# Moving the making of attention operand pieces from VectorE to GpSimd in a four-layer transformer kernel

## The reference

```
q, k, v = split of x @ w                        # per attention, heads of 8 features
s = q @ k^T (scaled)                            # attention 1 causal, 2 with distance slopes,
p = exp(s - max(s))                             # 3 with one more "void" key
y = (p @ v) / sum(p)
x = layernorm(x + y @ w_out)                    # float32 throughout
```

## Time and profile before

| | before |
|---|---|
| median of 3 runs | 1156.0 us |
| profiled execution | 1151.48 us, span 1149.7 us |
| PE busy | 981.2 us (85%) |
| DVE busy | 780.3 us (68%) |
| ACT busy | 660.3 us (57%) |
| POOL busy | 352.5 us (31%) |
| 12 first subtractions on DVE (L1557) | 14.9 us, 1240 ns each |
| 12 casts on DVE (L1559) | 9.3 us, 773 ns each |
| 12 second subtractions on DVE (L1561) | 14.7 us, 1226 ns each |

### The profile page before, as it was taken

One profiled execution on the slowest core, in us unless ns is written; L12 is line 12 of the kernel. 1 busy time (PEld: TensorE's weight loads), 2 busy tenths in 40 slices (PEclk: granted clock), 3 DMA queues, 4 the chain that ended last, 5 costly groups with the idle time before them and its releaser, 6 DMA issues.

```text
span 1149.7 us, 18859 instructions
## 1 busy us (share of the span) xinstructions
PE 981.2 (85%) x6456; PEld 500.3 (44%) x6517; DVE 780.3 (68%) x1663; ACT 660.3 (57%) x1282; POOL 352.5 (31%) x541
## 2 busy tenths in 40 slices
PE   5599779999887799446999999898899998888992
PEld 2266544445445588422333333476322222225661
DVE  5976596767752401389788887346988888855875
ACT  4755636665565254152677677584277766685451
POOL 7625510111342335520000001131021222645764
PEclk9799889999999899776999999989699999998996
DMA  5920224343631220233333210002334432411332
GB/s 141 175 68 1 69 84 162 122 134 111 152 88 47 59 60 25 62 102 130 98 121 129 77 63 31 2 1 82 106 105 147 133 103 78 112 29 47 97 102 84
DMA packets 98375, 101.70 MB, mean 88 GB/s; under 512 B 13354, under 2 KB 80571, under 8 KB 98199
## 3 DMA queue, kind: packets, MB, share of 16 engines
q1 hardware_dynamic: 86169, 89.28, 26.7%
q0 software_dynamic: 6432, 8.18, 2.5%
q10 hardware_dynamic: 5680, 3.04, 1.0%
HBM read 66.60 MB, written 38.09 MB: 91 GB/s over the span
## 4 chain that ended last, share of the span: by engine, by line
PE 66%; DVE 17%; ACT 6%; issue 5%; DMA 3%; POOL 2%; SPq 0%; another core or an unknown queue 0%; ACTq 0%; POOLq 0%; DVEq 0%
PE PS L894 13%; PE PS L878 12%; PE PS L851 8%; DVE negm L1696 6%; PE PS L705 5%; PE PS L700 5%; PE PS L1063 3%; PE PS L1073 3%; PE PS L881 3%; PE PS L1193 3%; PE PS L854 2%; PE PS L902 2%; ACT arena L1323 2%; PE PS L1208 2%; ACT arena L1250 2%
## 5 line engine op out<-in xcount | busy, mean ns | idle before, releaser
L1323 ACT ACTIVATE arena<-PS 128x512 f32<-128x512 f32 (+3 forms) x768 | 362.3, 549 | 185.5 <-PE PS L881 118.6
L1696 DVE TENSOR_REDUCE negm<-PS 128x2 f32<-128x1024 f32 (+3 forms) x384 | 404.5, 1087 | 88.1 <-PE PS L851 46.1
L878 PE MATMUL PS<-arena 128*128 128x512 bf16 (+3 forms) x707 | 218.7, 361 | 8.6 <-ACT arena L1323 5.4
L894 PE MATMUL PS<-arena,VPAD 128*32 128x512 f32 (+3 forms) x1536 | 186.3, 556 | 0.1
L851 PE MATMUL PS<-arena 32*128 32x512 bf16 (+3 forms) x768 | 143.9, 374 | 33.2 <-DVE negm L1696 28.1
L851 PEld LDWEIGHTS PS<-arena 32*128 32x128 bf16 x768 | 36.3, 91 | 215.0 <-DVE negm L1696 112.2
L878 PEld LDWEIGHTS PS<-arena 128*128 128x128 bf16 x768 | 69.7, 98 | 117.9 <-issue 54.2
L2533 POOL CAST nmp<-negm 128x16 bf16<-128x16 f32 x48 | 9.3, 195 | 360.1 <-DVE negm L1696 240.3
L700 PE MATMUL PS<-arena,W 128*128 128x512 f32 x144 | 81.4, 698 | 10.9 <-ACT arena L1241 8.5
L705 PEld LDWEIGHTS PS<-W,arena 128*128 128x128 f32 x640 | 79.6, 203 | 13.4 <-issue 6.7
L705 PE MATMUL PS<-W,arena 128*128 128x128 f32 x640 | 81.4, 288 | 3.3 <-DVE arena L1640 3.0
(11 more groups left out here) (335 smaller groups left out, 1538.8 us busy)
## 6 DMA issues: line engine op xcount, KB each, us to landing
arena<-score_q SPq DMA_DIRECT2D x48, 288.0 KB
arena<-score_k SPq DMA_DIRECT2D x48, 288.0 KB
arena<-max_parts SPq DMA_DIRECT2D x48, 256.0 KB
max_parts<-arena SPq DMA_DIRECT2D x36, 256.0 KB, 2.9
score_k<-arena SPq DMA_DIRECT2D x36, 128.0 KB
score_q<-arena SPq DMA_DIRECT2D x12, 384.0 KB
arena<-rows_y SPq DMA_DIRECT2D x16, 256.0 KB, 4.1
arena<-slots SPq DMA_DIRECT2D x46, 65.0 KB, 1.9
```

Source lines behind the costliest of these rows:

```text
L878: mm = pe.matmul(PS[:, b, q0:S], OK[s][:, r, kt * P:(kt + 1) * P], OQ[s][:, r, q0:S], start=True, stop=True)
L894: mm = pe.matmul(PS[32 * r:32 * r + 32, 7, q0:S], VP[:, u, kt, r, :], PB[:, kt % 2, r, q0:S], start=(kt == 0), stop=True, skip_group_check ...
L1323: act.activation(PB[:, kt % 2, r, q0:S], PS[:, 4 + use % 3, q0:S], ACT.Exp, scale=slope(u % G, r) if o["slope"] else 1.0).then_inc(exped, 1)
L1696: vec.tensor_reduce(negm[:, u % 2, 2 * rp:2 * rp + 2, qt], PS[:, 2 * (use % 2):2 * (use % 2) + 2, 0:nk], AX.X, ALU.max, negate=True).then_ ...
```

## The change

The three instructions of `splits` are made by GpSimd for chunks 1, 2 and 3 of every attention. Chunk 0's stay on VectorE. In GpSimd's stream chunk 1's three come in front of the first slots of lead, behind the last layer norm's roots. Those of chunks 2 and 3 come at slots 5, 7, 13 (chunk 2) and 15, 21, 23 (chunk 3). SP's spills and GpSimd's bias additions now wait on GpSimd for chunks 1 to 3.

```diff
+SPLIT_SLOTS = {5: (2, "lo"), 7: (2, "mid"), 13: (2, "low"), 15: (3, "lo"), 21: (3, "mid"), 23: (3, "low")}
...
-LAYER0_GPSIMD_TURNS = "01230130213020R011212323RR3RRRRRRR"
+LAYER0_GPSIMD_TURNS = "01230130213020R011212323RR31RRRRRRR023"
...
             def max_spills(c, tag, a):
-                sp.wait_ge(*V.at(c, tag + ".mid"))
+                sp.wait_ge(*(PO if c else V).at(c, tag + ".mid"))
...
             def score_spills(c, tag, a):
-                sp.wait_ge(*V.at(c, tag + ".low"))
+                sp.wait_ge(*(PO if c else V).at(c, tag + ".low"))
...
                     elif step == "split":
-                        splits(c, "p1")
+                        if c == 0:
+                            splits(c, "p1")
...
+            def split_low(c, tag):
+                L = lanes[c]
+                pool.wait_ge(*A.at(c, tag + ".k"))
+                pool.tensor_tensor(L.pair, L.pair, L.parts[:, :, 0, :], ALU.subtract).then_inc(*PO.did(c, tag + ".lo"))
+
+            def split_middle(c, tag):
+                L = lanes[c]
+                pool.wait_ge(*PO.at(c, tag + ".lo"))
+                pool.tensor_copy(L.parts[:, :, 1, :], L.pair).then_inc(*PO.did(c, tag + ".mid"))
+
+            def split_last(c, tag):
+                L = lanes[c]
+                pool.wait_ge(*PO.at(c, tag + ".mid"))
+                pool.tensor_tensor(L.parts[:, :, 2, :], L.pair, L.parts[:, :, 1, :], ALU.subtract).then_inc(*PO.did(c, tag + ".low"))
+
+            def first_splits(c, tag):
+                if c == 1:
+                    split_low(c, tag)
+                    split_middle(c, tag)
+                    split_last(c, tag)
...
+                    if t in SPLIT_SLOTS:
+                        c, piece = SPLIT_SLOTS[t]
+                        {"lo": split_low, "mid": split_middle, "low": split_last}[piece](c, f"p{a + 1}")
```

More of the change, by code:

```diff
@@ L92, in numbered @@
     return " ".join(f"{name}{i}" for i in range(n))
+SPLIT_STEPS = words(" ".join(f"p{a}.lo p{a}.mid p{a}.low" for a in (1, 2, 3)))
+SPLIT_SLOTS = {5: (2, "lo"), 7: (2, "mid"), 13: (2, "low"), 15: (3, "lo"), 21: (3, "mid"), 23: (3, "low")}
 NORM_V = "{0}.bn {0}.mv {0}.ln"
@@ L114 @@
 GPSIMD_STEPS = words(" ".join([
-    "m.va m.rs m.va2 m.rs2 m.lva m.lrs t.va t.rt t.rs t.s2 t.s1 t.va2 t.rt2 t.rs2 t.lva t.lrs o1.lva o1.lrs",
-    "x0.id x1.id cb.lva cb.lrs o2.xb o2.lva o2.lrs ch.xb ch.lva ch.lrs o3.xb r3.id r3.lva r3.lrs r3.nm r3.nb o3.lva o3.lrs r3.sh e.lva e.lrs"]))
+    "m.va m.rs m.va2 m.rs2 m.lva m.lrs t.va t.rt t.rs t.s2 t.s1 t.va2 t.rt2 t.rs2 t.lva t.lrs p1.lo p1.mid p1.low o1.lva o1.lrs",
+    "x0.id x1.id cb.lva cb.lrs p2.lo p2.mid p2.low o2.xb o2.lva o2.lrs ch.xb ch.lva ch.lrs p3.lo p3.mid p3.low o3.xb r3.id r3.lva r3.lrs r3.nm r3.nb o3.lva o3.lrs r3.sh e.lva e.lrs"]))
 TENSOR_STEPS = words(" ".join([
@@ L143 @@
 LAYER0_VECTOR = words("ss xn decay memory y x1 ss2 xn2 tot ln t.xn ssp t.tot t.ln split values")
-LAYER0_GPSIMD = words("rs rs2 lrs hh t.rs2 t.lrs")
+LAYER0_GPSIMD = words("rs rs2 lrs hh t.rs2 t.lrs split")
 LAYER0_TENSOR_TURNS = "0002300313202301332120112311001003201313131230102023220201310132121201202332011331RRR2RR2R2RR3R3RRRR3R"
@@ L153 @@
 COMBINE_VECTOR, COMBINE_VECTOR_TURNS = words("tot ln split values"), "010313021201RR3RRRRRRRR32RRR2R"
-COMBINE_GPSIMD, COMBINE_GPSIMD_TURNS = words("rs"), "R0RR132RRRRRRR"
+COMBINE_GPSIMD, COMBINE_GPSIMD_TURNS = words("rs split"), "R0RR1321RRRRRRR023"
 LAYER2_TENSOR, LAYER2_TENSOR_TURNS = words("o.tr o.out c.tr c.s c.out p.tr p.qk p.v p.vs"), "13103202110302312020101310021RR2R3RRRR2R3RRR3R32RR"
@@ L157 @@
 LAYER2_VECTOR, LAYER2_VECTOR_TURNS = words("o.tot o.ln c.tot c.ln split values scores"), "1310203211002021310103RRRRRR2R2RRR3R323RRR"
-LAYER2_GPSIMD, LAYER2_GPSIMD_TURNS = words("o.rs c.xb c.rs"), "103201120RRR233RRRRRRR"
+LAYER2_GPSIMD, LAYER2_GPSIMD_TURNS = words("o.rs c.xb c.rs split"), "103201120RRR2331RRRRRRR023"
 def rest(turns):
@@ L166, with __init__ @@
 class Steps:
-    def __init__(self, sem, engine, chunk_steps, whole_steps, last_only=()):
+    def __init__(self, sem, engine, chunk_steps, whole_steps, last_only=(), split=range(B)):
         self.sems = [sem(f"{engine}_chunk{c}") for c in range(B)] + [sem(f"{engine}_whole")]
-        self.order = [[name for name in chunk_steps if c == B - 1 or name not in last_only] for c in range(B)] + [whole_steps]
+        self.order = [[name for name in chunk_steps if (c == B - 1 or name not in last_only) and (c in split or name not in SPLIT_STEPS)]
+                      for c in range(B)] + [whole_steps]
         self.number = [{name: i + 1 for i, name in enumerate(steps)} for steps in self.order]
@@ L206, in sem @@
             return ctx.enter_context(nc.semaphore(name))
-        V = Steps(sem, "vector", VECTOR_STEPS, VECTOR_WHOLE, words("x1.y0 x1.y1 x1.y2"))
+        V = Steps(sem, "vector", VECTOR_STEPS, VECTOR_WHOLE, words("x1.y0 x1.y1 x1.y2"), range(1))
         A = Steps(sem, "scalar", SCALAR_STEPS, SCALAR_WHOLE)
-        PO = Steps(sem, "gpsimd", GPSIMD_STEPS, GPSIMD_WHOLE)
+        PO = Steps(sem, "gpsimd", GPSIMD_STEPS, GPSIMD_WHOLE, (), range(1, B))
         T = Steps(sem, "tensor", TENSOR_STEPS, TENSOR_WHOLE, words("o1.tr o1.out r1.tr r1.lg x1.o0 x1.o1 x1.o2 o3.tr o3.out r3.tr r3.lg"))
@@ L2009, in combine_and_prep @@
                     elif step == "split":
-                        splits(c, "p2")
+                        if c == 0:
+                            splits(c, "p2")
                     else:
@@ L2033, in layer2 @@
                     elif step == "split":
-                        splits(c, "p3")
+                        if c == 0:
+                            splits(c, "p3")
                     elif step == "values":
@@ L2370, in layer0 @@
                         root_of_sum(c)
+                    elif step == "split":
+                        first_splits(c, "p1")
                     else:
@@ L2439, in combine @@
                         continue
-                    norm(c, "cb")
+                    if step == "split":
+                        first_splits(c, "p2")
+                    else:
+                        norm(c, "cb")
             def layer2(slot):
                 for c in range(B):
-                    pool.wait_ge(*V.at(c, "p2.low"))
+                    pool.wait_ge(*(PO if c else V).at(c, "p2.low"))
                     biased(c, "o2", b2p)
@@ L2449, in layer2 @@
                         continue
-                    if step == "o.rs":
+                    if step == "split":
+                        first_splits(c, "p3")
+                    elif step == "o.rs":
                         norm(c, "o2")
@@ L2490, in inside3 @@
                 if t in BIAS_SLOTS:
-                    pool.wait_ge(*V.at(BIAS_SLOTS[t], "p3.low"))
+                    pool.wait_ge(*(PO if BIAS_SLOTS[t] else V).at(BIAS_SLOTS[t], "p3.low"))
                     biased(BIAS_SLOTS[t], "o3", b3o)
```

## The result

The changed kernel is not faster, it is a little slower. Its median was 1157.7 us (1154.49 to 1163.45, 11 runs) beside 1154.58 us for the kernel before (1147.19 to 1157.81, 11 runs): ratio 1.0047, 95% interval 1.0026 to 1.0067. Run again on another chip, it was 1180.11 against 1177.21 us, ratio 1.0025 (1.0002 to 1.0049). Later experiments ran on three chips, called by their numbers on record: 4, 9 and 5. On chips 9 and 5 the stretch behind attention 3 took 145 to 147 us in every profile; on chip 4 and in the first result it took 130 to 131 us. So times are compared within one job, and jobs by their ratios. The prediction was a gain of 3.4 us.

What follows compares the result with a forecast made beforehand. It took the VectorE-busy leads ahead of each attention as the bound, PE filling the slots. Terms 0 + 2.3 + 1.6 - 0.5 = 3.4 us took the profiled 1151.5 to 1148.1, median 1152.5 us, range 1145 to 1159.

Steps and rivals of the forecast that it cites:

- the norm ahead of attention 1: Lead of attention 1: layer norm passes two instructions per gap between GpSimd's, ending at 157.4 us instead of 155.5.
- the 159: Lead of attention 1: if the norm ends later than 159 us, the rival that norms are locked out decides.
- the norms are locked out: Rival: GpSimd's queued instructions leave VectorE no gaps in leads and attention 3's slots; 5.5 us slower, 1161.5; chance 0.12.
- Attention 3's lead: nothing: Ahead of attention 3: removed splits ran beside PE work and VectorE still waits for PE; gain 0.
- Attention 2: 2.3 us: Lead of attention 2: without the second split VectorE starts job 10 at 532.0 instead of 534.3; gain 2.3 us.
- held through all three: Lead of attention 2: a norm held through all three GpSimd instructions costs 2 us, leaving a gain of 0.3.
- Attention 1: 1.6 us: Lead of attention 1: of 6.2 us removed, the last copy of v starts near 166.0 against 167.6; gain 1.6 us.
- no hold-up at all gives 3.2: Bound for attention 1's lead: a norm not held up gains 3.2 us, with the max_rows wait remaining.
- The bound below, -0.8: Lead of attention 1: no norm instruction passes until GpSimd's third ends, at 159.8; 0.8 us slower.
- The slots: 0.5 us: Attention 3's slots: division at a unit's end held by up to 2.4 us, twice; charged 0.5 us, between 0 and 3.
- The range: Whole kernel: 1145 to 1159 us, from attention bounds (3.2 + 2.6) and run-to-run spread below, mild lock above.
- The prices on GpSimd: GpSimd's pieces, 1024 columns: two-operand subtraction 2.38 us, cast 1.05 us with 2.38 as upper bound.

Runs made afterwards that it cites:

- both: Changed kernel with chunk 1's pieces at slot -4 and attention 3's pieces moved away from the divisions; 1144.61 us, ratio 0.9927 to the kernel before.
- both_again: The kernel of both, run again on chip 9: 1165.6 us, ratio 0.9917 to the kernel before.
- c1_late: Changed kernel with chunk 1's three GpSimd instructions at slot -4, behind the first row of maxima; 1151.01 us, ratio 0.9982 to the kernel before.
- after_again: The changed kernel as it is, run again on chip 5: 1180.11 us against 1177.21 for the kernel before, ratio 1.0025.
- away_only: Changed kernel with only attention 3's pieces moved away from the divisions, chunk 1's left in place; 1174.38 us, ratio 0.9979 to the kernel before.
- behind_norm: Changed kernel with one wait added, so GpSimd starts chunk 1's three instructions after the norm; 1174.42 us against 1176.02 before, ratio 0.9989.
- only_23: Changed kernel with only chunks 2 and 3 on GpSimd, chunk 1 back on VectorE; 1150.44 us, ratio 0.9979 to the kernel before.
- pe_busy: Changed kernel with 24 unused products on PE during its wait for chunk 3's norm in attention 1's lead; 1179.26 us, ratio 1.0025 to before.
- only_c1: Changed kernel with only chunk 1's pieces on GpSimd, chunks 2 and 3 back on VectorE; 1163.34 us against 1152.47 before, ratio 1.0077.
- halves_again: The kernel of halves, run again on chip 5 beside the changed kernel: 1172.41 us, ratio 0.9971 to the kernel before.
- halves: Changed kernel with chunk 1's three GpSimd instructions each cut in two, six in the same place; 1172.94 us, ratio 0.9985 to the kernel before.

## Why the prediction was wrong

**The step that failed** is the norm ahead of attention 1: "two pass at 156.1 and two at 157.2, and the norm ends at 157.4 instead of 155.5". It was drawn from the row at 113.39 in the earlier trace rows, four instructions in 4.24 us, which I read as two getting through in the gap between GpSimd's instructions. The trace of before has the single durations of that row (min, median and max in ns, then the first and the last start):

```profile
L1551 DVE TENSOR_SCALAR X<-arena,mv,rs x4: 342/882/2384, 113.4 to 116.2; 128x128 f32<-128x128 f32 x4
```

GpSimd's addition began at 113.75 and ended at 116.20. The middle two sum to twice the median, 1.76 us. So two had started ahead of it (0.34 us each), one was held for its whole length (2.38), and the last started at 116.2 and took the remaining 1.42 us, held by the addition of 512 columns behind it. One instruction passes at the gap, not two. The changed kernel has the same, at its first lead, where one ended just behind the end of each of GpSimd's three (about 154.5, 155.6 and 157.8) and the fourth at 158.1:

```profile
L1555 DVE TENSOR_SCALAR X<-arena,mv,rs x4: 336/1251/2282, 153.2 to 157.7; 128x128 f32<-128x128 f32 x4
```

With one at a gap the prediction's own numbers (start 154.44, gaps at 156.0, 157.1 and 159.5) put the norm's end at 159.8. That is past the 159 that I had named as the point from which the rival decides. The evidence was in the trace of before, behind a group's mean. The rival "the norms are locked out" described what happened: 5.5 us slower by its price, 3.1 and 2.9 us measured in the medians (5.4 and 2.9 by the ratios). It had the division and PE's clock at other prices, so that the sum came near is in part luck.

**Attention 3's lead: nothing.** Without a held norm it is right (+0.22 and +0.19 us in `both` and `both_again`). In the changed kernel, chunk 3's norm took 4.99 us and cost +0.99; the rival had said up to 2.

**Attention 2: 2.3 us.** With the norm free the lead is 1.3 and 1.6 us shorter (`both`, `both_again`), so about two thirds of the term came. The missing part is on PE's timeline of `both`: the projections of chunk 3 at the lower clock (granted clock 0.50 until 522.0, before until 520.5).

```profile
518.87 3.45 PE L705 MATMUL PS<-arena,W 128*128 128x512 f32 x4
522.26 0.40 PE L856 MATMUL PS<-arena 32*128 32x512 bf16 x4
```

VectorE, freed of its split, waited 4.02 us there, and started its seven reductions at 522.69, no earlier than before ("about 522.3"). In the changed kernel nothing at all is left. The norm took 5.70 us to 514.79, and I had let it off as "still before the first maxima product". Queued behind it on VectorE are the eight additions of v (1.56 us in the chain), so the first reduction started at 516.40. The bound for a norm "held through all three", that "the gain there falls to 0.3", had it right.

**Attention 1: 1.6 us.** With the norm free, counted from the first reduction of maxima to score job 0, the lead is 3.2 us shorter in `both` (18.56 against 21.79), the bound "no hold-up at all gives 3.2"; in `c1_late` it is 3.7 and in `both_again` 4.8 us shorter. In the changed kernel it is 1.3 us longer (23.12). Counted from the norm's own start, score job 0 comes after 14.63 us before, 15.97 in the changed kernel (15.44 and 15.22 in `after_again` and `away_only`), and 9.62 to 12.59 in the five executions of kernels whose norm was free (`behind_norm`, `only_23`, `c1_late`, `both`, `both_again`). The bound below, -0.8, left out PE's clock behind the wait, which costs 2.3 (1.12 and 3.78 against 0.66 and 1.94).

**The slots: 0.5 us.** Right in kind ("That can be held by up to 2.4 us, twice") and too small: 2.83 and 0.77 us for two divisions, and 1.8 us more for rows 2 to 13, 3.5 in `c1_late`. "DVE idles a little between jobs" did not cover it, since PE stood still too. PE's timeline of the changed kernel, with the job that came next once the division was done:

```profile
850.83 0.39 PE L855 MATMUL PS<-arena 32*128 32x512 bf16 x2 [1.99 <-DVE arena L1733]
```

**The range.** It adds 3.2 and 2.6 us as the full bounds of the two attentions. The 2.6 is worked out nowhere: for attention 2 the text has 2.3, and 0.1 taken as 0.

**What held.** The prices on GpSimd (2.13 and 1.04 us; 2.38 and 1.05 predicted), reductions and additions from PSUM untouched, `max_rows` on time, nothing gained in the slots of attentions 1 and 2.

**The lock.** The section of the Trainium skill that the prediction drew on ("SBUF — State Buffer", "SBUF: two separate sides") calls it exclusive and whole-instruction. The traces agree: 2.28 us is the longest that an instruction of these three norms took, beside GpSimd instructions of 2.12. At each change of GpSimd's instructions one instruction of the norm got through; at the one change beside the division none did.

**Still open.** Rows 13 to 16 of attention 3 were 2.3 us longer. PE's granted clock fell there to 0.50 for some 10 us, in the changed kernel and again in `after_again` and `pe_busy`, and for some 3 us in `away_only` and `only_c1`. Those are the five executions whose norms take over 4 us; the two with the short fall are those without a held division. Between 940 and 1030 us it stayed at 1.00 in all eight others, the kernel before among them. Windows of the changed kernel (us, busy PE, PEld, DVE, ACT, POOL, clock, DMA share, GB/s):

```profile
970.00:975.00 5.00, 3.44 (x20) 0.67 (x18) 4.76 (x14) 3.21 (x6) 0.00 (x0) 1.00 0.29 91
975.00:980.00 5.00, 3.10 (x28) 0.98 (x29) 4.48 (x12) 1.83 (x5) 1.34 (x5) 0.64 0.20 76
980.00:985.00 5.00, 5.00 (x20) 1.56 (x20) 3.46 (x8) 2.17 (x4) 2.07 (x6) 0.50 0.05 10
```

PE had waited much there (3.44 us busy of 5 in the stretch before, 3.10 in the one in which it fell). `halves_again` has 2.94 us busy of 5 at the same work and no drop. Whether an earlier delay of a few microseconds decides it, and how, was not tested. It may be why `halves` and `both` gained more than their leads show.

## What to carry to other kernels

Before work is moved to GpSimd, list what VectorE does from SBUF to SBUF in the same microseconds, and count at most one VectorE instruction per gap between GpSimd's: a chain of four short ones beside three long ones costs nearly all three. Where the move puts them matters more than how much is moved: the same nine chunks' pieces took 1.0047 or 1.0025 of the time at one place, and 0.9927 or 0.9917 at another, away from the norms and divisions. If the place can't be changed, cut the long GpSimd instructions in two, or let GpSimd wait for the norm; with either the kernel was no longer slower than before. And when a row groups several instructions, read their single durations before a pattern is drawn from the sum.

## What the runs showed of the hardware

- GpSimd's cast of 128x1024 float32 to bf16 takes 1.04 us, its subtraction of two operands of that size 2.13 us; VectorE needs 0.77 and 1.24. Each half of 128x512 takes 0.61 and 1.15 us.
- A VectorE instruction of 0.34 us took up to 2.28 us beside them, a division of 0.29 us took 2.83. With PSUM on one side, three reductions (2.68 us) and an addition (0.30 us) kept their time.
- After a wait of 3.96 us for the norm PE came back at the lower of its two clock levels (granted clock 0.50, 1.2 GHz); kept busy through the wait, it stayed at the higher (1.00, 2.4 GHz). The windows of the changed kernel and then of `pe_busy`, over the projections of chunk 3 (columns as in the windows above):

```profile
160.00:163.60 3.60, 3.60 (x4) 1.09 (x4) 0.66 (x2) 1.08 (x2) 0.41 (x2) 0.50 0.05 20
```

```profile
161.80:163.60 1.80, 1.80 (x4) 0.64 (x4) 0.13 (x1) 0.68 (x2) 0.17 (x1) 1.00 0.05 18
```
